# Attention with int8 query projection: the query made transposed, keys and queries stacked through DRAM

## The chip, the cores and the metric

The kernel runs on one core of a Trainium2 chip. The metric is the device time in microseconds of one launch. PE is the matrix engine (PEld its weight loads), DVE the vector engine, ACT the scalar engine, POOL the general-purpose engine and SP the engine that issues nearly all transfers. A value in f32 that is to be multiplied at better than the rounded precision is split into a rounded part "hi" and a rest "lo"; a product is then three matmuls (hi·hi, hi·lo, lo·hi) or, where the inner size is only 32, one matmul over a stack of three 32-row pieces.

## The reference, cut to what matters

There are 32 batches of 112 tokens with 512 channels, 16 heads of 32, and a context of 375 rows a batch. The linear maps for q and for the output quantise both operands to integers in -127..127.

```python
def _w8a8_linear(x, w, b):
    qx, sx = _dyn_quant(x)            # a scale for each token
    qw, sw = _quant_weight(w)         # a scale for each output channel
    y = jnp.einsum('bnc,oc->bno', qx, qw) * (sx * sw[:, 0])
    return y + b
q = _w8a8_linear(x, wq, bq).reshape(B, N, H, D).transpose(0, 2, 1, 3)
k = (cond @ wk.T + bk).reshape(B, L, H, D).transpose(0, 2, 1, 3)
v = (cond @ wv.T + bv).reshape(B, L, H, D).transpose(0, 2, 1, 3)
scores = jnp.einsum('bhnd,bhld->bhnl', q, k) * inv_sqrt_d + mask[:, None]
attn = jax.nn.softmax(scores, axis=-1)
o = jnp.einsum('bhnl,bhld->bhnd', attn, v)
return _w8a8_linear(o, wo, bo)
...
x = x + attention(_layernorm(x), ctx_2048, mask)
x = x + ffn(_layernorm(x))            # 8 experts, top 2 of them a token
```

## The kernel before

The program has four stages, one after the other: `prepare_weights` (weights of q and of the output quantised and turned, those of k and v split), `attention`, `route` and `experts`. The change touches the first two.

`attention` is a software pipeline over the batches, written by hand. Iteration `it` runs the heads of batch `it` (scores, softmax, turned probabilities, values), prepares batch n = `it`+1 (its projections of k and v, its q), loads and normalises x of batch `it`+2, and finishes the batches `it`-1 and `it`-2 (output projection, second normalisation, router). Every engine runs its own list of instructions, ordered by the head number h = 0..15; between engines only semaphores count. Each engine's list is executed strictly in its order, SP's list of transfers too. Iterations -1 and before only fill the pipeline, iterations 32 and 33 empty it, and iteration 31 has no next batch to prepare.

The path of q of batch n, before. DVE quantises the normalised x to `x_int` (112 tokens in partitions) at h = 14 of the iteration before. PE turns it at h = 6 (L603), DVE clips it to `x_int_t`, and PE multiplies at h = 7 (L638): four bf16 matmuls with 512 columns, tokens in partitions. DVE multiplies by the token's scale (one number a partition) and the row `wq_row` at h = 8 (L498), POOL adds `bq_row` (L357), PE turns the result at h = 9 with four f32 transposes (L603), ACT rounds it to `q_hi` out of `misc` at h = 9 (L424), and DVE makes `q_lo` at h = 10 (L502). Now the channels are in partitions, four groups of 128, which are four heads of 32 rows each.

A score is one matmul over 96 rows, so SP gathers 32-row pieces: `k_stack` holds k_hi, k_lo, k_hi and `q_stack` q_hi, q_hi, q_lo. `stack_keys(half)` issues 12 transfers for eight heads (L279), from SBUF to SBUF, each of 32 partitions and two heads; two halves a batch. The queries take 12 more (L316). That is 36 transfers a batch on SP, besides the twelve others (weights of the experts that are split on the way in four parts, mask, x, context, results). The first half of the keys of batch n may be overwritten once the eighth score of `it` is done, the second half once all sixteen are.

The lines that bind one engine to the other here: `scores` on PE waits for `k_stacked` and `q_stacked` at h = 0 and for `k_stacked` at h = 8; ACT waits for `k_stacked` before it overwrites `k_hi` and for `q_stacked` before it overwrites `q_hi`.

## Time and profile before

| | |
|---|---|
| median of 3 runs | 1607.95 us (1605.15 to 1608.63) |
| profiled execution, its own time | 1609.71 us |
| its span, first to last instruction | 1608.0 us |
| PE busy | 1494.6 us, 93% of the span |
| DVE, ACT, POOL busy | 897.5, 884.0, 660.6 us |
| mean granted clock of PE | 0.965 of full |

Full speed of PE is 2.4 GHz, and the other level that occurs is half of it. Matmuls overlap in the record, so the sum of their durations says less than the distance from one start to the next. In the rows below a time is in microseconds from the start of the span.

### The profile page before, as it was taken

Reading aid. Unit: us, or ns where it says so; the run is one execution under the profiler, and the core shown is the slowest. Engines: PE = TensorE matmul, PEld = TensorE weight load, DVE = VectorE, ACT = ScalarE, POOL = GpSimd, SP = SyncE. Lnnn points to the kernel's source line nnn. Section 1 sums busy time; section 2 is a strip of 40 time slices with the busy share of each in tenths; the row PEclk is TensorE's granted clock in tenths of the full one; section 3 lists DMA queues with packets and bytes.
Section 4 is the critical chain, followed back from the end, with each engine's and each line's share of the span. In section 5 each row is a group of like instructions: output and inputs, shape, how many; then the busy total and the mean of one; then the engine's idle time right before and its main releaser. Section 6 shows DMA issues by size and latency. Waiting matters only on the chain. (4 is left out here: it accounts for less than half of the span.)

```text
span 1608.0 us, 40123 instructions
## 1 busy us (share of the span) xinstructions
PE 1494.6 (93%) x11594; PEld 1317.6 (82%) x11595; DVE 897.5 (56%) x2365; ACT 884.0 (55%) x2097; POOL 660.6 (41%) x671
## 2 busy tenths in 40 slices
PE   2899999999999999999999999984399999999896
PEld 2788888888888888888888888873299999999895
DVE  6557666766676667666766676654632222222221
ACT  2467667677777776777677767761033333333232
POOL 4233334333443234323432343323555555656453
PEclk9999999999999999999999999985599999999998
DMA  5567777677767776777677767654537776666643
GB/s 173 145 170 196 209 200 197 179 228 205 194 178 226 202 196 179 225 205 196 178 225 201 200 179 222 185 142 141 160 68 186 182 175 134 148 154 125 160 77 48
DMA packets 220124, 281.09 MB, mean 175 GB/s; under 512 B 83568, under 2 KB 164976, under 8 KB 220080
## 3 DMA queue, kind: packets, MB, share of 16 engines
q1 hardware_dynamic: 203952, 247.24, 54.3%
q0 software_dynamic: 16128, 33.30, 11.6%
q8 instruction: 23, 0.38, 0.1%
q14 instruction: 21, 0.17, 0.0%
HBM read 118.31 MB, written 66.17 MB: 115 GB/s over the span
## 5 line engine op out<-in xcount | busy, mean ns | idle before, releaser
L464 DVE CUSTOM_DVE_ANT_0 probs<-score,neg_mask 112x375 f32<-112x375 f32 x512 | 279.7, 546 | 254.8 <-PE score L555 251.5
L392 ACT ACTIVATE probs<-probs,neg_max 112x375 f32<-112x375 f32 x512 | 312.3, 610 | 197.2 <-DVE neg_max L464 191.7
L563 PE MATMUL turn<-ident,probs 112*125 112x112 f32 x1536 | 264.8, 282 | 2.8 <-ACT probs L392 2.5
L385 ACT ACTIVATE probs_t<-turn 125x336 f32<-125x336 f32 x512 | 226.0, 441 | 71.6 <-PE turn L563 70.6
L563 PEld LDWEIGHTS turn<-ident,probs 112*125 112x125 f32 x1536 | 227.2, 190 | 36.4 <-issue 14.4
L555 PE MATMUL score<-k_stack,q_stack 96*112 96x376 f32 x512 | 209.4, 409 | 8.5 <-DMA q_stack<-q_lo 6.2
L591 PE MATMUL proj<-ctx_hi,wk_hi 128*128 128x376 f32 x512 | 176.0, 344 | 1.9 <-PEq L29 1.1
L591 PE MATMUL proj<-ctx_lo,wk_hi 128*128 128x376 f32 x512 | 172.0, 336 | 0.0
L591 PE MATMUL proj<-ctx_hi,wk_lo 128*128 128x376 f32 x512 | 171.7, 335 | 0.0
L1032 DVE TENSOR_TENSOR a_lo<-a_ps,a_hi 128x384 fp32r<-128x384 f32 x63 | 35.1, 557 | 243.7 <-ACT a_hi L1007 243.7
L596 PE MATMUL proj<-wv_hi,ctx_hi 128*125 128x512 f32 x384 | 151.8, 395 | 0.0
L596 PE MATMUL proj<-wv_hi,ctx_lo 128*125 128x512 f32 x384 | 151.7, 395 | 0.0
L596 PE MATMUL proj<-wv_lo,ctx_hi 128*125 128x512 f32 x384 | 151.0, 393 | 0.0
L354 POOL TENSOR_SCALAR neg_mask<-neg_mask 112x375 f32<-112x375 f32 x32 | 16.8, 525 | 305.2 <-DMA neg_mask<-mask 305.2
L370 POOL TENSOR_TENSOR ctx_lo<-ctx_stage,ctx_hi 128x1504 fp32r<-128x1504 f32 x31 | 106.6, 3437 | 57.9 <-ACT ctx_hi L429 57.9
L990 POOL DMA_INDIRECT out<-y_rows,scatter_idx x63 | 101.9, 1618 | 57.3 <-POOL scatter_idx L986 50.7
L375 POOL TENSOR_TENSOR w_raw<-w_raw,w_hi 128x1056 fp32r<-128x1056 f32 x32 | 78.9, 2467 | 92.9 <-ACT w_hi L434 92.9
L591 PEld LDWEIGHTS proj<-ctx_hi,wk_hi 128*128 128x128 f32 x512 | 97.4, 190 | 8.7 <-issue 1.5
L1020 ACT ACTIVATE y_rows<-y_ps,row_share 128x512 f32<-128x512 f32 x63 | 43.5, 691 | 106.7 <-PE y_ps L1102 73.3
L555 PEld LDWEIGHTS score<-k_stack,q_stack 96*112 96x112 f32 x512 | 92.4, 181 | 9.9 <-issue 7.5
L591 PEld LDWEIGHTS proj<-ctx_lo,wk_hi 128*128 128x128 f32 x512 | 97.6, 191 | 0.0
L591 PEld LDWEIGHTS proj<-ctx_hi,wk_lo 128*128 128x128 f32 x512 | 96.9, 189 | 0.0
(198 smaller groups left out, 3393.9 us busy)
## 6 DMA issues: line engine op xcount, KB each, us to landing
k_stack<-k_hi SPq DMA_DIRECT2D x512, 94.0 KB, 2.2
k_stack<-k_lo SPq DMA_DIRECT2D x256, 94.0 KB, 2.2
ctx_stage<-ctx_t SPq DMA_DIRECT2D x32, 750.0 KB, 5.0
q_stack<-q_hi SPq DMA_DIRECT2D x256, 56.0 KB, 2.0
w_raw<-gate_up_t SPq DMA_DIRECT2D x32, 352.0 KB, 3.1
gate_up_dram_hi<-w_hi SPq DMA_DIRECT2D x32, 352.0 KB, 4.8
gate_up_dram_lo<-w_raw SPq DMA_DIRECT2D x32, 352.0 KB, 5.2
gate_up_hi<-gate_up_dram_hi SPq DMA_DIRECT2D x16, 704.0 KB, 4.9
```

The lines of the kernel that those rows point to most:

```text
L370: pool.tensor_tensor(c_lo[:, par % 2, :, :], stage[:, :, :], c_hi[:, par % 2, :, :].bitcast(F32), ALU.subtract).then_inc(c_lo_made, 1)
L375: pool.tensor_tensor(w_lo[:, :], w_raw[:, :], w_hi[:, :].bitcast(F32), ALU.subtract).then_inc(w_lo_made, 1)
L385: act.activation(probs_t[:, h % RING_T, :, :], turn[h % 2][0:LC, 0:LT * N].rearrange("p (l n) -> p l n", l=LT), ACT.Copy).then_inc(turned_ ...
L392: act.activation(probs[:, h % DS, :], probs[:, h % DS, :], ACT.Exp, bias=neg_max[:, par % 2, h:h + 1], scale=-1.0, accum_out=total[:, par ...
L464: dve.tensor_tensor_reduce(probs[:, h % DS, :], score[h % 2][0:N, 0:L], neg_mask[:, p, :], 1.0, BIG, ALU.add, ALU.min, neg_max[:, p, h:h + ...
L555: pe.matmul(score[h % 2][0:N, 0:LP], q_st[:, par % 2, h, :], k_st[:, h, :], start=True, stop=True).then_inc(scored, 1)
L563: mm = pe.transpose(turn[h % 2][0:LC, l * N:(l + 1) * N], probs[:, h % DS, l * LC:(l + 1) * LC], W["ident"][0:N, 0:N])
L591: mm = pe.matmul(bank[:, 0:LP], W[w][:, t, 128 * u:128 * u + 128], c[:, q, t, :], start=(t == 0 and w == "wk_hi" and c is c_hi), stop=(t = ...
L596: mm = pe.matmul(bank[0:LC, :], c[:, q, t, l * LC:(l + 1) * LC], W[w][:, t, :], start=(t == 0 and w == "wv_hi" and c is c_hi), stop=(t == ...
L990: pool.indirect_dma_start(out, bass.IndirectOffsetOnAxis(ap=si[par][:, 0:1], axis=0), y[:, par, :], None, compute_op=ALU.add).then_inc(sca ...
L1020: act.activation(y[:, other, :], y_ps[other][:, 0:C], ACT.Copy, scale=share[:, other:other + 1]).then_inc(y_made, 1)
L1032: dve.tensor_tensor(a_lo[:, :], a_ps[:, 0:FP], a_hi[:, :].bitcast(F32), ALU.subtract).then_inc(a_lo_made, 1)
```

## The change

q is made with the channels in partitions from the start: for each of the four channel groups four matmuls whose weights are a 128x128 piece of `wq_int` and whose moving operand is the turned `x_int_t` with 112 columns. The token's scale then varies along the free axis, so it is needed as a row in every partition: SP stores the 112 scales of batch `it`+2 to DRAM (`x_scales`) at the end of iteration `it`, fetches them back as a broadcast row in the next iteration, and POOL multiplies them by the channels' scale `wq_col` into `q_scale`. DVE multiplies by `q_scale`, POOL adds the column `bq_col`, and ACT and DVE split `q_t` out of SBUF instead of out of PSUM. The four f32 transposes at h = 9 go.

Keys and queries are kept as one tile of both parts (`k_parts`, `q_parts`), stored to DRAM (one transfer a half of the keys, one for the queries) and fetched back in three transfers each, one for each third of the stack. In all 12 transfers a batch take the place of 36, and two more move the scale. The heads lie in the stack in the order h % 4 * 4 + h // 4. ACT waits for `k_kept` and `q_kept` (stored) where it waited for the stacks. In `prepare_weights` the row `wq_row` (four spread activations, four f32 matmuls, one copy) goes, and the row `bq_row` becomes a column. DVE's list gets 14 semaphore increments ahead of its loop.

```diff
@@ prepare_weights, PE @@
-                pe.wait_ge(spread_done, KT * (i + 1))
-                if i:
-                    pe.wait_ge(row_out, i)
-                for t in range(KT):
-                    mm = pe.matmul(ps[0:N, 128 * t:128 * t + 128], spread[:, i, t, :], W["ident"][:, :],
-                                   start=True, stop=True)
-                mm.then_inc(row_made, 1)
+            pe.wait_ge(spread_done, KT)
+            for t in range(KT):
+                mm = pe.matmul(ps[0:N, 128 * t:128 * t + 128], spread[:, t, :], W["ident"][:, :],
+                               start=True, stop=True)
+            mm.then_inc(row_made, 1)
...
@@ attention, SP @@
-            def stack_keys(half):
-                for i in range(4):
-                    rows = slice(QUARTER * i, QUARTER * i + QUARTER)
-                    for r, src in ((0, k_hi), (1, k_lo), (2, k_hi)):
-                        sp.dma_start(k_st[QUARTER * r:QUARTER * r + QUARTER, 8 * half + i:8 * half + 8:4, :].bitcast(F32),
-                                     src[rows, 2 * half:2 * half + 2, :].bitcast(F32)).then_inc(k_stacked[half], 16)
+            def keep_keys(b, half):
+                sp.dma_start(k_dram[b, half, :, :, :], k_parts[:, :, 2 * half:2 * half + 2, :].bitcast(F32).rearrange("p a g l -> p a (g l)")).then_inc(k_kept[half], 16)
+            def stack_keys(b, half):
+                for r, part in ((0, 0), (1, 1), (2, 0)):
+                    sp.dma_start(k_st[QUARTER * r:QUARTER * r + QUARTER, :, :].bitcast(F32).rearrange("p (i g) l -> p i g l", g=G4)[:, :, 2 * half:2 * half + 2, :],
+                                 k_dram[b, half, :, part, :].rearrange("(i p) (g l) -> p i g l", p=QUARTER, g=2)).then_inc(k_stacked[half], 16)
...
                 if has_a:
-                    need(sp, unit_out, UNITS * it + KT)
+                    need(sp, k_kept[1], 16 * (it + 1))
                     if inside or it > 0:
                         waited(sp)
                         need(sp, scored, H * it)
-                    stack_keys(1)
+                    stack_keys(it, 1)
...
+                if has_n:
+                    need(sp, x_scale_stored, 16 * (n + 1))
+                    need(sp, q_scaled, n)
+                    sp.dma_start(x_scale_row[:, :], x_scales[n, :].rearrange("(a t) -> a t", a=1).to_broadcast([128, N])).then_inc(x_scale_in, 16)
...
                     need(sp, unit_out, UNITS * n + KT // 2)
+                    keep_keys(n, 0)
+                    need(sp, k_kept[0], 16 * (n + 1))
                     if has_a:
                         waited(sp)
                         need(sp, scored, H * it + H // 2)
-                    stack_keys(0)
+                    stack_keys(n, 0)
+                    need(sp, unit_out, UNITS * n + KT)
+                    keep_keys(n, 1)
                     need(sp, q_out, 3 * n + 3)
-                    for i in range(4):
-                        rows = slice(QUARTER * i, QUARTER * i + QUARTER)
-                        for r, src in ((0, q_hi), (1, q_hi), (2, q_lo)):
-                            sp.dma_start(q_st[QUARTER * r:QUARTER * r + QUARTER, q, i:H:4, :].bitcast(F32),
-                                         src[rows, :, :].bitcast(F32)).then_inc(q_stacked, 16)
+                    sp.dma_start(q_dram[n, :, :, :], q_parts[:, :, :, :].bitcast(F32).rearrange("p a g n -> p a (g n)")).then_inc(q_kept, 16)
+                    need(sp, q_kept, 16 * (n + 1))
+                    for r, part in ((0, 0), (1, 0), (2, 1)):
+                        sp.dma_start(q_st[QUARTER * r:QUARTER * r + QUARTER, q, :, :].bitcast(F32).rearrange("p (i g) n -> p i (g n)", g=G4),
+                                     q_dram[n, :, part, :].rearrange("(i p) f -> p i f", p=QUARTER)).then_inc(q_stacked, 16)
...
+                if has_nn:
+                    nn = it + 2
+                    need(sp, ln1, 8 * nn + 5)
+                    with nc.allow_non_contiguous_dma(reason="one scale a token"):
+                        sp.dma_start(x_scales[nn, :].rearrange("(p a) -> p a", a=1), x_scale[:, par % 2:par % 2 + 1]).then_inc(x_scale_stored, 16)
...
@@ attention, POOL @@
+                    need(pool, x_scale_in, 16 * (n + 1))
+                    need(pool, q_out, 3 * n)
+                    pool.tensor_tensor(q_scale[:, :, :], x_scale_row[:, :].unsqueeze(1).to_broadcast([128, G4, N]),
+                                       W["wq_col"][:, :].unsqueeze(2).to_broadcast([128, G4, N]), ALU.mult).then_inc(q_scaled, 1)
                     need(pool, q_out, 3 * n + 2)
-                    need(pool, q_made, 3 * n)
-                    pool.tensor_tensor(q_tok[:, :], q_tok[:, :], W["bq_row"][0:N, :], ALU.add).then_inc(q_biased, 1)
+                    pool.tensor_tensor(q_t[:, :, :], q_t[:, :, :], W["bq_col"][:, :].unsqueeze(2).to_broadcast([128, G4, N]),
+                                       ALU.add).then_inc(q_biased, 1)
...
@@ attention, ACT, h == 9 @@
-                        need(act, q_made, 3 * n + 3)
-                        need(act, q_stacked, 16 * QDMAS * n)
-                        act.activation(q_hi[:, :, :], misc[:, 0:G4 * N].rearrange("p (g n) -> p g n", g=G4),
-                                       ACT.Identity).then_inc(q_hi_made, 1)
+                        need(act, q_biased, n + 1)
+                        need(act, q_kept, 16 * n)
+                        act.activation(q_hi[:, :, :], q_t[:, :, :], ACT.Identity).then_inc(q_hi_made, 1)
...
@@ attention, DVE, h == 8 and ahead of the loop @@
-                        dve.scalar_tensor_tensor(q_tok[:, :], misc[0:N, :], x_scale[:, q:q + 1], W["wq_row"][0:N, :],
-                                                 ALU.mult, ALU.mult).then_inc(q_out, 1)
+                        need(dve, q_scaled, n + 1)
+                        dve.tensor_tensor(q_t[:, :, :], misc[:, 0:G4 * N].rearrange("p (g n) -> p g n", g=G4), q_scale[:, :, :],
+                                          ALU.mult).then_inc(q_out, 1)
...
+            for _ in range(LOOP_OFFSET):
+                waited(dve)
...
@@ attention, PE, h == 7 and 9 @@
-                        for t in range(KT):
-                            mm = pe.matmul(misc[0:N, :], x_int_t[:, t, :], W["wq_int"][:, t, :], start=(t == 0), stop=(t == KT - 1))
+                        for g in range(G4):
+                            for t in range(KT):
+                                mm = pe.matmul(misc[:, g * N:(g + 1) * N], W["wq_int"][:, t, 128 * g:128 * g + 128], x_int_t[:, t, :],
+                                               start=(t == 0), stop=(t == KT - 1))
                         mm.then_inc(q_made, 1)
-                    if h == 9 and has_n:
-                        need(pe, q_biased, n + 1)
-                        turn_to_misc(lambda t: q_tok[:, 128 * t:128 * t + 128], W["ident"][0:N, 0:N], misc, N, 128).then_inc(q_made, 1)
```

On PE the order moves at h = 7 to 10. Before, in the first iteration with scores (L638 is the q product, L603 the transposes, L563 the turned probabilities, L555 the scores, L591 and L596 the projections of k and v):

```order
L638 MATMUL misc<-wq_int,x_int_t 112x512 x4
L563 MATMUL turn<-ident,probs 125x112 x3
L555 MATMUL score<-k_stack,q_stack 112x376
...
L596 MATMUL proj<-wv_hi,ctx_hi 125x512
L596 MATMUL proj<-wv_lo,ctx_hi 125x512
L596 MATMUL proj<-wv_hi,ctx_lo 125x512
L603 MATMUL misc<-ident,q_tok 128x112 x4
L563 MATMUL turn<-ident,probs 125x112 x3
L555 MATMUL score<-k_stack,q_stack 112x376
```

and now (L667 is the q product, L591 the turned probabilities, L583 the scores, L624 the projection of v):

```order
L667 MATMUL misc<-x_int_t,wq_int 128x112 x16
L591 MATMUL turn<-ident,probs 125x112 x3
L583 MATMUL score<-k_stack,q_stack 112x376
...
L624 MATMUL proj<-wv_hi,ctx_hi 125x512
L624 MATMUL proj<-wv_lo,ctx_hi 125x512
L624 MATMUL proj<-wv_hi,ctx_lo 125x512
L591 MATMUL turn<-ident,probs 125x112 x3
L583 MATMUL score<-k_stack,q_stack 112x376
```

Sixteen short matmuls stand in the place of four long ones, and nothing stands between the last projection of v of h = 9 and the turned probabilities of h = 10.

On SP one whole iteration, here iteration 2, which is written out ahead of the loop. Before, from the last transfer ahead of the keys on; the nine rows of keys of the second half that come before L292 read like the nine that follow L304:

```order
L292 DMA w_raw<-gate_up_t 128x704
L293 DMA w_raw<-down_t 128x352
L296 DMA neg_mask<-mask 112x375
L299 DMA out<-y 112x512
L301 DMA h_rows<-h_s 112x512
L304 DMA x_res<-x 112x512
L279 DMA k_stack<-k_hi 32x2x376
...
L316 DMA q_stack<-q_hi 32x4x112 x2
L316 DMA q_stack<-q_lo 32x4x112
...
L321 DMA ctx_stage<-ctx_t 128x4x375
L323 DMA x_in<-x 112x512
```

and now, from the row of the scales to the end of the iteration, less the four stores of the split expert weights (L341 and L342):

```order
L311 DMA x_scale_row<-x_scales 128x112
L314 DMA x_res<-x 112x512
L280 DMA k_parts_dram<-k_parts 256x1x752
L285 DMA k_stack<-k_parts_dram 32x4x752 x3
L280 DMA k_parts_dram<-k_parts 256x1x752
L327 DMA q_parts_dram<-q_parts 128x896
L330 DMA q_stack<-q_parts_dram 32x4x448 x3
L335 DMA ctx_stage<-ctx_t 128x4x375
L337 DMA x_in<-x 112x512
...
L347 DMA x_scales<-x_scale 112x1
```

The store of the second half of the keys stands behind the fetch of the first; the fetch of the queries stands directly behind their store, for which SP waits; the scales are stored last.

## Rows read from the trace of the kernel before

**Rows 1.** Stretches: busy us (count) of PE, PEld, DVE, ACT, POOL; clock; DMA share; GB/s.

```profile
59.18:1063.00 1003.82, 996.78 (x8590) 861.83 (x8591) 681.38 (x1925) 707.88 (x1759) 354.00 (x300) 1.00 0.71 197
579.58:611.85 32.27, 32.25 (x282) 27.78 (x281) 22.32 (x64) 23.02 (x57) 11.73 (x10) 1.00 0.73 198
557.00:558.00 1.00, 1.00 (x9) 1.00 (x7) 0.56 (x2) 1.00 (x4) 0.00 (x0) 1.00 0.65 153
...
59.00:65.00 6.00, 5.82 (x20) 5.84 (x21) 1.67 (x6) 2.21 (x6) 0.00 (x0) 0.50 1.02 283
```

**Rows 2.** What PE waited for, 62 to 1060 us: us in total, times, longest.

```profile
PE score L555 <- DMA q_stack<-q_lo: 2.6, 3, 1.3
PE misc L603 <- POOL q_tok L357: 1.8, 2, 1.4
PE score L555 <- issue: 1.7, 2, 1.3
```

**Rows 3.** PE in order of time: start, us, what, count.

```profile
560.32 0.37 PE L603 MATMUL misc<-ident,x_int 112*128 112x112 bf16 x4
560.53 0.54 PE L563 MATMUL turn<-ident,probs 112*125 112x112 f32 x3
...
561.59 1.02 PE L638 MATMUL misc<-wq_int,x_int_t 128*112 128x512 bf16 x4
562.46 0.48 PE L563 MATMUL turn<-ident,probs 112*125 112x112 f32 x3
...
565.40 0.40 PE L596 MATMUL proj<-wv_lo,ctx_hi 128*125 128x512 f32 x1
565.64 0.40 PE L596 MATMUL proj<-wv_hi,ctx_lo 128*125 128x512 f32 x1
565.98 0.60 PE L603 MATMUL misc<-ident,q_tok 112*128 112x112 f32 x4
566.42 0.49 PE L563 MATMUL turn<-ident,probs 112*125 112x112 f32 x3
```

**Rows 4.** Weight loads into misc: shortest, median, longest duration in ns.

```profile
L603 PEld LDWEIGHTS misc<-ident,x_int x128: 97/98/102, 43.8 to 1044.1; 112*128 112x128 bf16 x128
```

**Rows 5.** SP's issues in the same iteration: start, us to issue.

```profile
549.94 0.63 SPq L279 DMA_DIRECT2D k_stack<-k_hi  x1
...
561.47 0.73 SPq L279 DMA_DIRECT2D k_stack<-k_hi  x1
...
569.39 1.24 SPq L316 DMA_DIRECT2D q_stack<-q_hi  x2
...
577.40 0.42 SPq L321 DMA_DIRECT2D ctx_stage<-ctx_t  x1
```

**Rows 6.** Transfers: count, KB each, median us from issue to landing.

```profile
k_stack<-k_hi SPq DMA_DIRECT2D x512, 94.0 KB, 2.2
...
gate_up_dram_hi<-w_hi SPq DMA_DIRECT2D x32, 352.0 KB, 4.8
...
x_res<-x SPq DMA_DIRECT2D x32, 224.0 KB, 4.4
```

**Rows 7.** The path of q outside PE, in the same iteration.

```profile
563.80 0.74 DVE L498 SCALAR_TENSOR_TENSOR q_tok<-misc,x_scale,wq_row 112x512 f32<-112x512 f32 x1
...
564.63 1.29 POOL L357 TENSOR_TENSOR q_tok<-q_tok,bq_row 112x512 f32<-112x512 f32 x1 [1.61 <-DVE q_tok L498]
...
567.77 0.62 DVE L502 TENSOR_TENSOR q_lo<-misc,q_hi 128x448 fp32r<-128x448 f32 x1
```

**Rows 8.** The start: weights prepared, q of batch 0, the first score.

```profile
29.31 1.99 PE L156 MATMUL w_ps<-ident,w_spread 128*112 128x128 f32 x8
31.09 1.06 PE L149 MATMUL w_pt<-ident,w_ints 128*128 128x128 bf16 x8
...
49.19 0.62 DVE L502 TENSOR_TENSOR q_lo<-misc,q_hi 128x448 fp32r<-128x448 f32 x1 [0.22 <-ACT q_hi L424]
...
59.18 0.63 PE L555 MATMUL score<-k_stack,q_stack 96*112 96x376 f32 x1 [3.60 <-DMA q_stack<-q_lo]
```

More of the change, by code:

```diff
@@ L39, in prepare_weights @@
         ints = sb("w_ints", [128, 2, KT, C], BF16)
-        spread = sb("w_spread", [128, 2, KT, N])
+        spread = sb("w_spread", [128, KT, N])
         ones = sb("w_ones", [128, N])
@@ L97, in _ @@
             act.wait_ge(ident_made, 3)
-            for i in range(2):
-                act.wait_ge(scale_done, i + 1)
-                for t in range(KT):
-                    act.activation(spread[:, i, t, :], ones[:, :], ACT.Copy, scale=scale[:, i, t:t + 1]).then_inc(spread_done, 1)
+            act.wait_ge(scale_done, 2)
+            for t in range(KT):
+                act.activation(spread[:, t, :], ones[:, :], ACT.Copy, scale=scale[:, 1, t:t + 1]).then_inc(spread_done, 1)
             act.wait_ge(W["ctx_in"], 16)
@@ L104, in _ @@
             act.activation(W["c_hi"][:, 0, :, :], W["stage"][:, :, :], ACT.Identity).then_inc(W["c_hi_made"], 1)
-            for i, (_, _, row) in enumerate(pairs):
-                act.wait_ge(row_made, i + 1)
-                act.activation(row[0:N, :], ps[0:N, :], ACT.Copy, scale=-inv_sqrt_d if i == 0 else 1.0).then_inc(row_out, 1)
+            act.wait_ge(row_made, 1)
+            act.activation(W["wo_row"][0:N, :], ps[0:N, :], ACT.Copy).then_inc(row_out, 1)
         @block.vector
         def _(dve):
-            for i, (n, _, _) in enumerate(pairs):
+            for i, (n, _) in enumerate(pairs):
                 dve.wait_ge(loaded[n], 16)
@@ L128, in _ @@
                                       ALU.subtract).then_inc(ints_done, 1)
-            for i, (_, dst, _) in enumerate(pairs):
+            for i, (_, dst) in enumerate(pairs):
                 for t in range(KT):
@@ L189, in attention @@
         stage, c_hi, c_lo, x_in = W["stage"], W["c_hi"], W["c_lo"], W["x_in"]
-        k_hi, k_lo = sb("k_hi", [128, G4, LP], F32R), sb("k_lo", [128, G4, LP], F32R)
+        k_parts = sb("k_parts", [128, 2, G4, LP], F32R)
+        k_hi, k_lo = k_parts[:, 0, :, :], k_parts[:, 1, :, :]
         k_st = sb("k_stack", [96, H, LP], F32R)
-        q_hi, q_lo = sb("q_hi", [128, G4, N], F32R), sb("q_lo", [128, G4, N], F32R)
+        q_parts = sb("q_parts", [128, 2, G4, N], F32R)
+        q_hi, q_lo = q_parts[:, 0, :, :], q_parts[:, 1, :, :]
         q_st = sb("q_stack", [96, 2, H, N], F32R)
@@ L203, in attention @@
         x_int, x_int_t = sb("x_int", [N, C], BF16), sb("x_int_t", [128, KT, N], BF16)
-        q_tok = sb("q_tok", [N, C])
+        q_t = sb("q_t", [128, G4, N])
+        x_scale_row, q_scale = sb("x_scale_row", [128, N]), sb("q_scale", [128, G4, N])
         out_ts = sb("out_ts", [128, G4, N])
@@ L547, in _, with stacked_at @@
         def _(pe):
+            def stacked_at(h):
+                return h % 4 * G4 + h // 4
             def scores(b, par, h):
@@ L554, in scores @@
                 need(pe, masked, k - 1)
-                pe.matmul(score[h % 2][0:N, 0:LP], q_st[:, par % 2, h, :], k_st[:, h, :],
+                pe.matmul(score[h % 2][0:N, 0:LP], q_st[:, par % 2, stacked_at(h), :], k_st[:, stacked_at(h), :],
                           start=True, stop=True).then_inc(scored, 1)
@@ L636, in body @@
                         need(pe, q_out, 3 * n + 1)
[L637 to L638 removed]
+                        for g in range(G4):
+                            for t in range(KT):
+                                mm = pe.matmul(misc[:, g * N:(g + 1) * N], W["wq_int"][:, t, 128 * g:128 * g + 128], x_int_t[:, t, :],
+                                               start=(t == 0), stop=(t == KT - 1))
                         mm.then_inc(q_made, 1)
[L640 to L642 removed]
                     if h == 11 and has_m:
```

37 lines of the change are left out of this document (20 added, 17 removed).

## The prediction

> **What bounds the kernel now.** I read first the stretches, then what PE waited for, then PE in order of time. In one iteration of the attention loop, 32.27 us long, PE is busy for 32.25 us, while ACT has 23.0, DVE 22.3 and POOL 11.7 us of work, and the transfer engines are busy for 0.73 of the time [rows 1]. The whole stretch from the first score to iteration 31 is 1003.8 us, or 32.4 us for each of its 31 iterations. PE's waits between 62 and 1060 us come to 6.1 us in these rows [rows 2], and the same view by shorter stretches has all of them in the first five iterations. After those the loop costs what its matmuls cost on PE, by start-to-start distance, and a microsecond taken from PE's list in one iteration counts 31 times, as long as no other chain closes up. After 1063 us the change touches nothing that carries time.
>
> The second nearly full resource is SP's list. In the iteration shown the 12 transfers of a half of the keys take from 561.47 to 569.39 and the 12 of the queries from there to 577.40, 7.9 and 8.0 us [rows 5]: 0.66 us for each issue, 23.9 us for all 36, and 12 other issues beside them. The queries are issued just before the next iteration's first score, at 579.58. That is why the waits of the first iterations are mostly for `q_stack`.
>
> **The change, part by part.** All sums are against the profiled execution's own 1609.71 us.
>
> (a) The transposes at h = 9. The last two matmuls of v start at 565.40 and 565.64, so the next could start at 565.88; the turned probabilities behind the transposes start at 566.42 [rows 3]. The transposes, with the wait for POOL's bias ahead of them, take 0.54 us. Removed from 31 iterations: 16.7 us. In iteration -1 they lie in front of a wait of 3.60 us [rows 8] and count nothing in PE's own order.
>
> (b) The q product. Before, 561.59 to 562.46, 0.87 us for four matmuls with 512 columns [rows 3]. Now 16 with 112 columns, each with its own 128-column bf16 weights. The trace has just this shape in the transposes of `x_int`: four from 560.32 to 560.53, 0.21 us, 0.0525 us each [rows 3]. 16 make 0.84 us: a gain of 0.03 an iteration, 0.9 us in all. From above, if the weight loads of 98 ns [rows 4] hid under nothing, 16 would take 1.57 us, a loss of 0.70 an iteration. From below 112 columns at the rate of the 512 (0.2175 us each) are 0.048 us, 0.76 in all. I take 0.84, since shape and type are the same.
>
> The Trainium skill speaks against it (TensorE: Matmul & The Clock Gate, Back-to-back issue gap): streams of weight load and matmul are said to sustain about 81 ns a matmul with 128 columns and 131 ns with 512. By it the product would go from 0.52 to an estimated 1.30 us. The rows have 0.87 for the first of these, and 52.5 ns for the short shape, so the sum goes by the rows.
>
> (c) The other engines' steps. DVE multiplies 128x448 in place of 112x512, about 0.65 for 0.74 us, POOL's bias is 1.13 for 1.29, by 448/512 of [rows 7], and POOL has a new product of the same size, 1.13 us more on 11.7. ACT's rounding no longer waits for PE. DVE and ACT have over 9 us of room an iteration. Cost nothing; the cover is PE's full list.
>
> (d) SP's list. 36 issues become 12, two small ones come in: some 22 x 0.66 = 14.5 us of SP's time come free in an iteration. In the steady loop that is worth nothing, as PE waits for none of it. In the first iterations it removes the lateness of the queries: of the 6.1 us in [rows 2] I take 5.5 (from 0, if new waits replace them, to 6.1).
>
> (e) The weights' stage. Of the f32 matmuls with `w_spread` at 29.31 the q part goes: until the next transposes at 31.09 that is 1.8 us [rows 8], on the chain transposes, output weights, last copy. 1.8 us.
>
> (f) The start of the loop. `q_lo` of batch 0 ends at 49.81 and the first score starts at 59.18 [rows 8], 9.4 us, of which 8 are SP's 12 issues. Now: a store, a wait, three fetches. A transfer lands after 2.2 us from SBUF to SBUF with 94 KB, and 4.8 us for a 352 KB store to DRAM beside others [rows 6]; the 448 KB store lies between, about 3.6, then two more issues of 0.66 and a last fetch of about 3. In all 7.9: a gain of 1.5 us (-1.6 to 3.7, with 4.8 or 2.2 for both).
>
> Sum: 16.7 + 0.9 + 5.5 + 1.8 + 1.5 = 26.4 us. The median lies 1.8 us below the profiled execution; taken from it, 1607.95 - 26.4 = 1581.6.
>
> **The new waits, and their room.** The iteration in the rows begins at 547.3 and the next at 579.58 [rows 1]. Keys, second half: stored in the iteration before, fetched from about 550, where their first issue stands now [rows 5], and needed at h = 8, at 562.5 [rows 3]. Room some 5 us. Keys, first half: fetch cannot start before the eighth score (561.4), as now [rows 5], needed at 579. Room over 10.
>
> The scales. Their fetch stands behind the second result store on SP, which needs DVE's h = 3, so at about 555.5; with 4.4 us to land as the neighbouring `x_res` has [rows 6] and 1.13 us on POOL the product is there at 561.1. DVE needs it at 563.80 [rows 7]. Room 2.7 us, and a late `q_t` first has to use up the room of the queries. Behind the waiting POOL instruction stand the bias, `x_res` and the norm of the next batch, all with room.
>
> The queries are the tight one. `q_lo` ends at 568.4 [rows 7]; PE wants them at 579.0 in the shorter iteration: 10.6 us for what took 9.4 at the start before and which I price at 7.9. Room 2.7 us. But the store now runs behind the keys' store, and the bytes grow: each iteration moves 2.0 MB more (1.54 of keys, 0.46 of queries) on 6.4 (198 GB/s by 32.27 us), 266 GB/s over 31.7 us. At 153 GB/s of 32-partition fetches the engines were busy for 0.65 [rows 1], so such fetches end near 235 GB/s, and all in all I get a DMA share near 0.95.
>
> **The rivals.**
>
> *Queries late (slower).* If a store and a last fetch each take the 4.8 us of the loaded store, the chain is 4.8 + 1.3 + 4.8 = 10.9 us, 0.3 over. If the 32-partition fetches out of DRAM run only at the 153 GB/s seen, 0.69 MB of queries take 4.5 us instead of 2.9 and the 1.16 MB of keys ahead 7.5 instead of 4.9, which pushes the store: 4.2 us more, 1.5 over the room. A stall of 1.5 us is 46 us in 31 iterations: 1582 + 46 = 1628. It decides from a chain of 11.2 us on, where the stall (0.6) eats (a) and (b). For it speaks the queue of bytes, against it that rows before have 283 GB/s in a crowded stretch [rows 1]. The Trainium skill (SBUF — State Buffer, Door 1: The DMA port swizzle) says that 32 partitions reach only half of the 16 ports. By its 436 GB/s for all I estimate 218 for such a fetch; the share of 0.65 at 153 GB/s agrees.
>
> *Weight loads not hidden.* (b) at its upper bound costs 0.70 an iteration, 21.7 us, in place of the 0.9 gained: 1582 + 22.6 = 1604.
>
> *Scales late.* Above 2.7 us of lateness DVE stands at h = 8, and its later scores with it. A fetch of 8 us would leave some 1 us of stall an iteration: 1582 + 31 = 1613.
>
> *The gain is hidden.* If the chain of score, DVE maximum, ACT exponential and turned probabilities closes up, only (e), (f) and part of (d) stay: 1608 - 8 = 1600. Against it: ACT 23.0 of 32.27.
>
> **How the numbers follow.** Forecast 0.72; queries late 0.13 (a third of it a small stall that leaves a gain); weight loads 0.06; scales late 0.04; hidden 0.05. The likeliest case alone is 1574 to 1592: 3.4 us below its sum if the half clock between 59 and 65 us [rows 1] does not come back once the wait of 3.6 us before the first score shrinks, 10 above if (d) gives nothing and (f) goes wrong. With the weight loads, the hidden gain and the small stalls the range is 1573 to 1604. Within 0.2%, 3.2 us, is about what a measurement of this kernel can tell from no change. Faster: 0.72, hidden 0.05, most of the weight loads 0.04, small stalls 0.04, 0.85. Slower: 0.11. Same: 0.04.
>
> **What would show it.** Right: an iteration of about 31.7 us with PE at 100%; the 16 matmuls 0.84 us from first start to next; no wait of a score for `q_stack` after the first iteration; SP waiting some 14 us an iteration more. Wrong: PE waits for `q_stack` in every iteration; a pitch of 80 to 98 ns in the q product; DVE waiting for POOL's `q_scale`; a DMA share of 1.

## The result, and the profile after

The changed kernel takes 1807.22 us (median of 4 runs, 1800.99 to 1808.19), the kernel before 1608.29 beside it: ratio 1.1231, interval 1.12 to 1.1262. It is 12% slower. The profiled execution took 1806.98 us, its span is 1805.2 us. The sum of the prediction, 1582, is 225 us too low. The experiments below split this into 153 us that go with the form of the scales' store, 46 us by which the kernel without that harm is still slower than the one before, and the 26 us of gain that did not come.

The stretches of the changed kernel; columns as in [rows 1]:

```profile
62.00:1256.00 1194.00, 1054.21 (x8841) 928.34 (x8841) 680.60 (x1927) 703.61 (x1762) 380.05 (x331) 0.93 0.82 220
609.68:645.58 35.90, 33.41 (x289) 29.43 (x289) 22.31 (x63) 23.02 (x57) 12.29 (x11) 0.94 0.86 233
...
644.00:651.00 7.00, 5.42 (x19) 5.38 (x20) 1.78 (x5) 2.08 (x7) 1.28 (x1) 0.57 1.04 346
645.60:647.00 1.40, 1.40 (x5) 1.35 (x6) 0.50 (x3) 0.00 (x0) 0.00 (x0) 0.50 0.99 281
...
653.00:654.00 1.00, 1.00 (x36) 0.83 (x24) 0.00 (x0) 0.15 (x1) 0.62 (x2) 1.00 0.28 87
```

An iteration that was full of PE work [rows 1] is now 35.90 us long in this example, with PE busy for 33.41. Two other things stand in the rows: a granted clock under 1, and a stretch in which the transfer engines are busy for only 0.28 of the time, though transfers of SP's are still on the way. The loop itself ends near 1256 us instead of 1063.

What PE waited for between 65 and 1265 us (us in total, times, longest):

```profile
PE score L583 <- DMA q_stack<-q_parts_dram: 94.7, 27, 8.5
PE score L583 <- issue: 18.8, 5, 4.8
PE misc L631 <- DVE o_int L471: 10.4, 11, 1.2
PE misc L655 <- ACT h_t L442: 8.3, 5, 3.2
PE proj L619 <- DVE k_parts L512: 5.5, 4, 1.9
```

The first two are one wait, that of the first score for its queries: 113.5 us where [rows 2] had 4.3. These five rows make 137.7 us. The rest is the clock: 0.93 over 1194 us, with 1.2 and 2.4 GHz as its two levels, is an estimated 167 us at the lower, in which half, about 84 us, is lost. Together 222 us, against a span that is 197 us longer than before and 224 longer than the forecast. The lower level follows the wait: PE is idle for 2.5 us before the score at 645.58, the next 1.4 us run at 0.50, and between 644 and 651 the mean is 0.57, that is, about 6 of the 7 us at the lower level.

What SP waited for, same stretch; the number behind each wait is again us in total, times, longest:

```profile
SPq L330 <- DMA q_parts_dram<-q_parts: 228.1, 31, 8.9
SPq L298 <- DMA down_dram_lo<-w_raw: 221.9, 25, 11.7
SPq L255 <- DMA k_parts_dram<-k_parts: 152.8, 31, 7.4
```

Three waits, 603 us, for a store to land. Two I had seen coming, those of the queries and of the keys. The middle one is the wait of the raw expert weights' load for the last store of the split ones; that edge existed before, and the change's diff does not touch it.

One iteration of SP, issue by issue (start, us to issue):

```profile
608.37 0.39 SPq L342 DMA_DIRECT2D down_dram_lo<-w_raw  x1
609.14 0.34 SPq L347 DMA_DIRECT2D x_scales<-x_scale  x1
609.67 2.15 SPq L285 DMA_DIRECT2D k_stack<-k_parts_dram  x3
620.24 0.35 SPq L298 DMA_DIRECT2D w_raw<-gate_up_t  x1
...
624.20 0.57 SPq L280 DMA_DIRECT2D k_parts_dram<-k_parts  x1
629.81 1.32 SPq L285 DMA_DIRECT2D k_stack<-k_parts_dram  x3
631.37 0.55 SPq L280 DMA_DIRECT2D k_parts_dram<-k_parts  x1
632.20 0.38 SPq L327 DMA_DIRECT2D q_parts_dram<-q_parts  x1
640.05 1.30 SPq L330 DMA_DIRECT2D q_stack<-q_parts_dram  x3
...
645.59 0.55 SPq L347 DMA_DIRECT2D x_scales<-x_scale  x1
646.98 1.40 SPq L285 DMA_DIRECT2D k_stack<-k_parts_dram  x3
657.38 0.35 SPq L298 DMA_DIRECT2D w_raw<-gate_up_t  x1
```

Read it from the top. The last weight store is issued at 608.37, and the load that waits for it leaves at 620.24, 11.9 us later; before, a store of this group landed after 4.8 us [rows 6]. Between the two stand only the scale store and the keys' fetch. In the next iteration it is the same, and there the window 653 to 654 shows the transfer engines busy for 0.28. Everything behind is late by that much: the keys' first half at 624.20, its fetch at 629.81. Then the queries: DVE's subtraction for `q_lo` starts at 631.3 and takes 0.62 us; the store of both parts is issued at 632.20 and has landed at 640.05, and the score starts at 645.58. From the end of `q_lo` that chain is 13.6 us, where 10.6 were to be had.

The scales' row is late as well. Its fetch is issued at 622.96, 13.3 us after the first score of the iteration, where the prediction had 8.2. DVE then stands before its product with `q_scale`, 65 to 1265 us:

```profile
DVE q_t L521 <- POOL q_scale L376: 53.7, 27, 4.7
```

Landings of the changed kernel, 62 to 1256 us (count, KB each, median us from issue to landing):

```profile
k_stack<-k_parts_dram SPq DMA_DIRECT2D x187, 376.0 KB, 5.4
k_parts_dram<-k_parts SPq DMA_DIRECT2D x62, 752.0 KB, 6.8
...
q_stack<-q_parts_dram SPq DMA_DIRECT2D x96, 224.0 KB, 3.7
q_parts_dram<-q_parts SPq DMA_DIRECT2D x31, 448.0 KB, 7.9
```

The matmuls did what was forecast. PE in order of time (start, us, what, count):

```profile
625.19 0.33 PE L619 MATMUL proj<-ctx_hi,wk_lo 128*128 128x376 f32 x1
625.37 0.96 PE L667 MATMUL misc<-x_int_t,wq_int 128*128 128x112 bf16 x16
626.16 0.54 PE L591 MATMUL turn<-ident,probs 112*125 112x112 f32 x3
```

16 matmuls in 0.79 us from the first's start to the next work, 49 ns each. Where the transposes stood, the turned probabilities now start 0.24 us after the last matmul of v (629.40 to 629.64), one ordinary distance.

### The profile page after: what moved, and what is told of

Its sections match the earlier page's. It is cut to its first block and busy times, and to the rows that moved or that the text cites. A ratio compares the mean times of both kernels' runs of the same rounds, so it can differ in the third digit from the quotient of the medians.

```text
span 1805.2 us, 40617 instructions
## 1 busy us (share of the span) xinstructions
PE 1552.8 (86%) x11842; PEld 1384.6 (77%) x11843; DVE 896.5 (50%) x2366; ACT 877.0 (49%) x2092; POOL 687.4 (38%) x703
## 5 line engine op out<-in xcount | busy, mean ns | idle before, releaser
L583 PE MATMUL score<-k_stack,q_stack 96*112 96x376 f32 x512 | 227.1, 443 | 115.0 <-DMA q_stack<-q_parts_dram 94.7
L591 PE MATMUL turn<-ident,probs 112*125 112x112 f32 x1536 | 281.5, 296 | 5.3 <-ACT probs L415 5.3
L591 PEld LDWEIGHTS turn<-ident,probs 112*125 112x125 f32 x1536 | 248.0, 205 | 31.6 <-issue 10.5
L619 PE MATMUL proj<-ctx_hi,wk_hi 128*128 128x376 f32 x512 | 194.9, 381 | 8.7 <-DVE k_parts L512 7.6
L583 PEld LDWEIGHTS score<-k_stack,q_stack 96*112 96x112 f32 x512 | 101.2, 198 | 120.9 <-issue 117.5
L619 PE MATMUL proj<-ctx_lo,wk_hi 128*128 128x376 f32 x512 | 188.4, 368 | 0.0
L619 PE MATMUL proj<-ctx_hi,wk_lo 128*128 128x376 f32 x512 | 187.5, 366 | 0.0
L624 PE MATMUL proj<-wv_hi,ctx_hi 128*125 128x512 f32 x384 | 152.8, 398 | 3.1 <-DVE k_parts L512 3.1
L624 PE MATMUL proj<-wv_hi,ctx_lo 128*125 128x512 f32 x384 | 152.4, 397 | 0.0
L624 PE MATMUL proj<-wv_lo,ctx_hi 128*125 128x512 f32 x384 | 152.1, 396 | 0.0
L619 PEld LDWEIGHTS proj<-ctx_hi,wk_hi 128*128 128x128 f32 x512 | 112.4, 220 | 17.7 <-DVE k_parts L512 9.2
L363 POOL TENSOR_TENSOR y<-y,x_res 112x512 f32<-112x512 f32 x32 | 40.9, 1278 | 219.2 <-DVE y L492 219.2
L619 PEld LDWEIGHTS proj<-ctx_lo,wk_hi 128*128 128x128 f32 x512 | 111.7, 218 | 0.0
L619 PEld LDWEIGHTS proj<-ctx_hi,wk_lo 128*128 128x128 f32 x512 | 109.9, 215 | 0.0
```

Source lines behind the costliest of these rows:

```text
L583: pe.matmul(score[h % 2][0:N, 0:LP], q_st[:, par % 2, stacked_at(h), :], k_st[:, stacked_at(h), :], start=True, stop=True).then_inc(scored, 1)
L591: mm = pe.transpose(turn[h % 2][0:LC, l * N:(l + 1) * N], probs[:, h % DS, l * LC:(l + 1) * LC], W["ident"][0:N, 0:N])
L619: mm = pe.matmul(bank[:, 0:LP], W[w][:, t, 128 * u:128 * u + 128], c[:, q, t, :], start=(t == 0 and w == "wk_hi" and c is c_hi), stop=(t = ...
L624: mm = pe.matmul(bank[0:LC, :], c[:, q, t, l * LC:(l + 1) * LC], W[w][:, t, :], start=(t == 0 and w == "wv_hi" and c is c_hi), stop=(t == ...
```

## Experiments

There were two suspects, the store of the scales (112 writes of 4 bytes into one piece of 448 bytes) and the stacks' way through DRAM, and a third question: whether the shorter PE list is worth anything. All times are medians; "before" is the kernel before on the same chip. It took 1604 to 1610 us in the five groups of runs, so a difference between runs of different groups is good to some 5 us only.

| run | scales | keys | queries | us | ratio to before (95%) |
|---|---|---|---|---|---|
| changed kernel | 4-byte store | DRAM | DRAM | 1807.22 | 1.12 to 1.1262 |
| e1_no_scale_store | none | DRAM | DRAM | 1653.81 | 1.023 to 1.0305 |
| e1_scale_own_rows | 4-byte, own rows | DRAM | DRAM | 1657.65 | 1.024 to 1.0317 |
| e4_after_turned_scale | 4 x 128 bytes | DRAM | DRAM | 1654.61 | 1.0242 to 1.0346 |
| e1_stacks_only | q as before | DRAM | DRAM | 1636.23 | 1.0088 to 1.0191 |
| e1_local_stacks | 4-byte store | SBUF | SBUF | 1664.77 | 1.0268 to 1.0386 |
| e3_before_plus_store | q as before, 4-byte store | SBUF | SBUF | 1659.31 | 1.0301 to 1.0368 |
| e2_local_no_store | none | SBUF | SBUF | 1608.76 | 1.0005 to 1.0036 |
| e2_scale_by_pe | by PE | SBUF | SBUF | 1610.92 | 1.002 to 1.0059 |
| e2_only_queries_dram | none | SBUF | DRAM | 1583.74 | 0.983 to 0.9902 |
| e2_only_keys_dram | none | DRAM | SBUF | 1586.57 | 0.9851 to 0.9926 |
| e3_pe_scale_q_dram | by PE | SBUF | DRAM | 1591.65 | 0.9879 to 0.9925 |
| e3_turned_scale_q_dram | 4 x 128 bytes | SBUF | DRAM | 1594.15 | 0.9885 to 0.993 |

### The scale store taken away, or its writes spread (e1_no_scale_store, e1_scale_own_rows)

The first drops the store and fetches the broadcast row from x instead, so that values of x stand in for the token scales. The second keeps 112 writes of 4 bytes, but gives each a DRAM row of its own, 512 bytes apart; its row too is fetched from x.

```diff
-sp.dma_start(x_scales[nn, :].rearrange("(p a) -> p a", a=1), x_scale[:, ...])   # both
+sp.dma_start(x_scales[nn, :, 0:1], x_scale[:, ...])                             # own rows only
-... x_scales[n, :] ... to_broadcast([128, N])
+... x[n, 0, 0:N] ... to_broadcast([128, N])
```

> The changed kernel without the store of the token scales; the row is fetched from x instead, so the scales of q are wrong ones and only the time counts. Theory 1 (the 112 writes of 4 bytes hold up the transfer queue for some 7 us an iteration, so the stores of the expert weights land late, the loads, the first half of the keys and the queries follow late): the attention loop falls to about 32 us an iteration and the whole to 1580 to 1620 us. Theory 2 (the 2 MB more an iteration and the fetches into 32 partitions out of DRAM are too slow by themselves): the time stays within 30 us of 1807.

> The scales are stored, each into a DRAM row of its own of 512 bytes, and the row is fetched from x as in the run without the store, so the scales of q are wrong ones. Theory 1a (the small writes disturb because they fall on the same 448 bytes): as without the store, 1580 to 1620 us. Theory 1b (each write of 4 bytes costs, wherever it falls): about 1800 us. Theory 2: about 1807 us.

1653.81 and 1657.65 us, both above the 1580 to 1620 of the expectation that had the store as the one cause: the store costs some 150 us here, and only in the form in which all its writes lie in one small piece. The waits of PE and of SP without the store, 65 to 1100 us:

```profile
PE score L577 <- DMA q_stack<-q_parts_dram: 35.0, 24, 3.5
PE score L577 <- issue: 11.6, 4, 3.2
```

```profile
SPq L329 <- DMA q_parts_dram<-q_parts: 194.1, 30, 8.0
SPq L255 <- DMA k_parts_dram<-k_parts: 130.8, 31, 5.7
SPq L298 <- DMA down_dram_lo<-w_raw: 109.0, 30, 4.9
```

The weights' wait falls from 8.9 us a time (221.9 in 25) to 3.6 (109.0 in 30). The waits for keys and queries fall only from 4.9 and 7.4 us to 4.2 and 6.5, and the first score is still late by 1.5 us an iteration. So there are two causes, and one is left.

### The transposed q with the old stacks, and the new stacks with the old q (e1_local_stacks, e1_stacks_only)

```diff
 # e1_local_stacks: 24 + 12 transfers from SBUF to SBUF as before, scales stored and fetched as in the change
-KDMAS, QDMAS = 3, 3
+KDMAS, QDMAS = 12, 12
 # e1_stacks_only: the kernel before with k_parts, q_parts and the 12 transfers through DRAM
-KDMAS, QDMAS = 12, 12
+KDMAS, QDMAS = 3, 3
```

> q made transposed with the scales through DRAM, but keys and queries stacked from SBUF to SBUF by 36 transfers a batch as before. Theory 1: the small writes still hold up the queue, the weights' stores land late and SP's full list gets later still: 1650 to 1850 us. Theory 2: with the DRAM stacks gone the transposed q is worth its 17 us: 1585 to 1595 us.

> q made as before (tokens in partitions, transposes, no scales through DRAM), keys and queries stacked through DRAM by the 12 transfers. Theory 1: no small writes, so the queue keeps up: 1595 to 1620 us. Theory 2: the DRAM stacks are the trouble: 1750 to 1830 us.

1664.77 and 1636.23 us: each half of the change is slower by itself than the kernel before (1609.89 us beside them), by 55 and by 26 us. For the second 1595 to 1620 us had been expected with the small writes as the one cause, so that is not the one cause either. In e1_stacks_only PE's first score waits 21 us in all for its queries, where it waits 46.6 in e1_no_scale_store, which has the transposed q besides. With both stacks through DRAM the transposed q thus costs 18 us (1636.23 to 1653.81) in place of a gain. The transposed q leaves a shorter iteration for the same chain and puts the fetch of the row on SP's list; which of these it is, no run took apart.

### The store alone, on the kernel before (e3_before_plus_store)

```diff
+if has_nn:
+    need(sp, ln1, 8 * nn + 5)
+    sp.dma_start(x_scales[nn, :].rearrange("(p a) -> p a", a=1), x_scale[:, ...]).then_inc(x_scale_stored, 16)
```

> The kernel before with one thing added: the store of 112 token scales, 4 bytes each, into one 448-byte piece of DRAM, at the end of SP's body; nothing fetches it, so the extra store changes nothing in the output. If such a store is dear by itself (my theory, since with each scale in a DRAM row of its own the changed kernel lost about 150 us of its time), what SP queues behind it (the raw weights' loads of the next iteration and the queries' transfers) lands 4 to 6 us later, and the time goes to 1630 to 1700 us. If the store is only dear where the bytes of keys and queries through DRAM keep the rings full, this run stays within 1605 to 1620 us (one more issue of 0.6 us on SP each iteration).

1659.31 us, 51 more than before (1608.31 beside it). PE's waits between 65 and 1100 us:

```profile
PE misc L610 <- POOL q_tok L364: 15.2, 16, 3.8
PE score L562 <- DMA k_stack<-k_hi: 11.7, 10, 3.4
PE score L562 <- DMA q_stack<-q_lo: 5.3, 6, 2.2
```

These waits make 32 us of the 51; the rest was not taken apart. SP has a wait that the kernel before does not have in its loop:

```profile
SPq L293 <- DMA down_dram_lo<-w_raw: 24.1, 16, 2.8
```

Nothing reads what is stored, and no instruction waits for it inside the loop; it is paid for by the transfers around it, here the last store of the weights, which SP issues just before it. Its rival, that the store hurts only where keys and queries through DRAM fill the queues, falls. Against the kernel before beside them, e1_local_stacks and e2_local_no_store (below) differ by 50 us too. So the store costs some 50 us where the stacks are made inside SBUF, and 150 where the landing of other stores is on the path three times an iteration. Not all of the 50 need be the form of the store: it is also one more issue, 0.65 us in the median, on a list of SP that has only 28 us to spare in 995 (below), by my estimate up to 20 us in 31 iterations. No run stored the scales in own rows or in four pieces beside stacks that are both made in SBUF.

### Is the shorter PE list worth its price? (e2_local_no_store, e2_only_queries_dram, e2_only_keys_dram)

All three have the transposed q and no scale store (values of x stand in for the token scales). The first has both stacks inside SBUF; each of the others sends one of them through DRAM.

```diff
 # e2_only_queries_dram against e2_local_no_store
-for i in range(4):
-    for r, src in ((0, q_hi), (1, q_hi), (2, q_lo)):
-        sp.dma_start(q_st[...], src[rows, :, :])
+sp.dma_start(q_dram[n, :, :, :], q_parts[:, :, :, :]).then_inc(q_kept, 16)
+need(sp, q_kept, 16 * (n + 1))
+for r, part in ((0, 0), (1, 0), (2, 1)):
+    sp.dma_start(q_st[...], q_dram[n, :, part, :])
```

> Both suspects taken away: keys and queries stacked from SBUF to SBUF, and the scales not stored (the row comes from x, so q's scales are wrong ones). Theory 1 (two separate costs, the shared small writes and the longer queue of the DRAM stacks): what is left is the transposed q, worth 17 to 20 us, 1588 to 1595 us. Theory 3 (something in the q path itself costs, POOL's new product or the order of the waits): 1605 us or more.

> Queries stacked through DRAM, keys from SBUF to SBUF, no store of the scales. If the queue of bytes ahead of the queries (1.16 MB of keys fetched into 32 partitions and 0.77 MB stored) is what makes them late, this is nearly as fast as the version with both local, 1585 to 1600 us. If the round trip of the queries is too long by itself, 1620 us or more.

> Keys stacked through DRAM, queries from SBUF to SBUF in 12 transfers, no store of the scales. If the keys' traffic ahead in the queue sets the queries' landing, they are late here too, since 8 us of issuing come on top: 1610 to 1650 us. If only the queries' own round trip mattered, 1585 to 1595 us.

1608.76, 1583.74 and 1586.57 us, beside 1604.29 for the kernel before. The first has PE's list shorter by the 17.6 us of (a) and (b) and gains none of it, against the expected 1588 to 1595. The view that explains it is SP's waits, for the kernel before from 65 to 1060 us,

```profile
SPq L279 <- PE score L555: 18.9, 34, 1.9
SPq L327 <- POOL w_raw L375: 6.5, 19, 0.8
```

and of e2_local_no_store, 65 to 1100 us.

```profile
SPq L283 <- PE score L571: 15.3, 26, 1.5
SPq L334 <- POOL w_raw L386: 14.4, 2, 14.0
```

In the 995 us of the first SP waits for 28 in all; its list is 97% full. (Of the 14.4 us in the last line 14.0 are one wait at the end of the loop.) A full list of SP reaches PE by a detour, which DVE's waits show, 65 to 1100 us, first e2_local_no_store, then e2_only_queries_dram:

```profile
DVE q_t L509 <- POOL q_scale L364: 74.1, 31, 3.6
DVE q_t L509 <- POOL q_scale L364: 25.8, 24, 2.2
```

The scales' row is fetched late on the full list, POOL's product and with it DVE come late, and PE waits 22.6 us between 65 and 1060, of which 14.1 are for DVE's `o_int`; with the queries through DRAM it waits 7.9. PE and SP are both the bound, and a step off PE's list pays only if SP's list gets shorter too. With 12 query issues turned into 4 it does, and 25 us appear. That the path of the transposed q costs by itself, the rival in the expectation, falls, since 1583.74 us has the same path. The number of issues and the way through DRAM change together in these runs, so that it is the number is argued from SP's waits. Either stack may go through DRAM for that, but not both. With the keys through DRAM and the queries in 12 transfers inside SBUF the time is 1586.57 us, not the 1610 to 1650 expected: small transfers behind the keys' bytes landed after 3.0 us in the median. SP in e2_only_queries_dram:

```profile
550.14 0.37 SPq L320 DMA_DIRECT2D q_parts_dram<-q_parts  x1
552.64 1.31 SPq L323 DMA_DIRECT2D q_stack<-q_parts_dram  x3
```

The queries' store has landed after 2.5 us, which is also its median there. With the keys ahead of it, and still without the scale store, the same store takes 6.7 us in the median and 7.9 in this iteration of e1_no_scale_store:

```profile
621.85 1.35 SPq L285 DMA_DIRECT2D k_stack<-k_parts_dram  x3
623.45 0.55 SPq L280 DMA_DIRECT2D k_parts_dram<-k_parts  x1
624.28 0.39 SPq L326 DMA_DIRECT2D q_parts_dram<-q_parts  x1
632.21 1.30 SPq L329 DMA_DIRECT2D q_stack<-q_parts_dram  x3
```

Ahead of it stand 1.155 MB of keys (three times 376 KB of 1024 bytes), fetched into pieces of 32 partitions, and a store of 0.770 MB (752 KB). The change's own trace gives their rates:

```profile
633.00:636.00 3.00, 3.00 (x19) 2.68 (x20) 1.80 (x5) 1.82 (x5) 2.42 (x1) 1.00 1.05 220
636.00:638.00 2.00, 2.00 (x12) 1.67 (x11) 1.90 (x7) 0.85 (x3) 1.00 (x1) 1.00 1.00 358
```

220 GB/s while the fetches fill the rings, 358 once the 128-partition store is under way. 1.155 MB at 220 GB/s are 5.3 us and 0.770 at 358 are 2.2 us, 7.4 in all, of which some has gone when the queries' store is issued; the queries' own 0.459 MB at 358 then take 1.3. Counted from the keys' fetch at 629.81, this estimate ends at 638.5, and the queries' store had landed by 640.05. The trace agrees with the Trainium skill (SBUF — State Buffer, Door 1: The DMA port swizzle), from whose half of the ports I had estimated 218 GB/s.

### A scale without small writes (e2_scale_by_pe, e3_pe_scale_q_dram, e3_turned_scale_q_dram, e4_after_turned_scale)

Two ways, each in the full function. Either ACT spreads the scale over 128 columns and one f32 matmul against the identity makes the row in every partition, with no transfer; or DVE turns the scale in blocks of 32, and four pieces of 128 bytes are stored and fetched as a row.

```diff
 # by PE, at h = 2 (e2: DVE's product at h = 3; e3: at h = 2)
+pe.matmul(misc[:, 0:N], x_scale_wide[:, :], W["ident"][0:N, 0:N], start=True, stop=True)
 # turned
+dve.transpose(x_scale_t[:, p, :], x_scale[:, p, :])
+sp.dma_start(x_scales[nn, :].rearrange("(p a) -> p a", a=32), x_scale_t[0:128:32, par % 2, :])
```

> A version that could beat both: transposed q, stacks from SBUF to SBUF as before, and the row of the scales made by one f32 matmul of the spread scale with the identity (0.2 us on PE) at h = 2, with no transfer of scales at all. An iteration should fall from 32.27 to some 31.9 us: 1608 - 31 x 0.37 - 1.8 = 1595 us, range 1588 to 1603.

> The full function: the queries made transposed, their scale row made on chip by one f32 matmul (0.31 us on PE) right before the product, keys stacked inside SBUF as before, queries stacked through DRAM. With the queries alone through DRAM and no scale made the time was 1583.7 us; the matmul, its eviction and one pitch more add 0.4 to 0.6 us an iteration, 31 times 12 to 19 us at most: 1590 to 1602 us. If SP's list is what held the same scale path with SBUF stacks at 1610.9, this run must be at least 10 us below that; if the scale path itself held it (k_lo late behind DVE's scale), it stays at 1605 to 1612 us.

> The full function: the token scale turned on VectorE so that it leaves as four pieces of 128 bytes, instead of 112 writes of 4 bytes, fetched back as a row an iteration later; keys stacked inside SBUF as before, queries stacked through DRAM. Theory (the 4-byte writes into the same 448 bytes cost about 150 us of the changed kernel's time, keys and queries together through DRAM the other 50): nothing of either is left and the gain that was predicted from PE's steps shows, 1583 to 1595 us. If it is any store of the scale ahead of the weights' loads that stalls the queue, whatever its pieces, 1620 us or more.

> The changed kernel whole, keys and queries both through DRAM, with one edit: the token scale leaves as four pieces of 128 bytes instead of 112 writes of 4 bytes into the same 448 bytes. Theory: the small writes cost what the run with a DRAM row for each scale gave back, so 1645 to 1665 us; what is then left over the kernel before, about 45 us, is the wait for queries behind the bytes of keys. Rival, any store of the scale at that place stalls the queue when the rings are full of keys' bytes: 1700 us or more.

1610.92, 1591.65, 1594.15 and 1654.61 us. The first has both stacks in SBUF and gains nothing, against the expected 1588 to 1603; the second is the same with the queries through DRAM and 19 us faster. That the first meets SP's list again is argued and not shown: it has no transfer of scales, and SP waits 40 us there for PE's scores. The two differ in DVE's place of the scale product too, so not all of the 19 us need be SP's. The last is the changed kernel with nothing but the scale's store in another form, and it gives back 153 us. Its PE waits, 65 to 1100 us:

```profile
PE score L588 <- DMA q_stack<-q_parts_dram: 33.8, 24, 3.4
PE score L588 <- issue: 9.9, 4, 3.2
```

These are 44 us, about as without any store (46.6): a store of the scale is free there if its pieces are few. With only the queries through DRAM it is not quite, 1594.15 beside 1583.74 us without a store, though on two chips. The best version of the full function is e3_pe_scale_q_dram, 1591.65 us (1591.24 to 1592.56), 1.0% under the kernel before; e3_turned_scale_q_dram, 1594.15 (1587.66 to 1596.24), can't be told from it.

## Why the prediction was wrong

**(a) and (b), PE's list: right.** The transposes are gone from PE's rows, and 16 matmuls take 0.79 us for the 0.84 forecast. The figure of the Trainium skill that I had weighed against it (TensorE: Matmul & The Clock Gate, Back-to-back issue gap, 81 ns for such a pair) is contradicted by the rows, 49 ns. The rival "weight loads not hidden" is out.

**(c), the other engines: nearly right in cost, shown by e2_only_queries_dram,** where a gain of 20.6 us (1583.74 beside a before of 1604.29) stands for the 26.4 of the sum. DVE's waits for `q_scale`, at nothing in the sum, are 25.8 us even there, and PE waits 7.9 us in all.

**(d), SP's list: two errors.** The first is "two small ones come in": the scale's store was counted as one issue of 0.66 us, by its 448 bytes. It cost 153 us in the changed kernel (e4_after_turned_scale, with the same bytes in four pieces) and 51 on the kernel before. This is the step that failed, and no rival of mine held it. "Scales late" priced the row's arrival, not what the store does to its neighbours. That rival came true as well, DVE waiting 53.7 us for `q_scale`, but as something that follows from SP's late list: with the scales in four pieces it waits 2.8 us (e4_after_turned_scale). How much of the 153 us goes by that way, no run shows. The second is "In the steady loop that is worth nothing": SP's list, 97% full, was as much the bound as PE's. With the stacks left alone (a) and (b) would have been worth nothing (1608.76). I had called SP's list nearly full and had not drawn the consequence. The change did free the list, so this error cost the sum nothing.

**"The new waits, and their room", the queries: the term was mis-sized.** I priced the chain from `q_lo` to score at 7.9 us with 10.6 to be had. It is 13.6 us in the changed kernel and, in the iteration of e1_no_scale_store shown above (`q_lo` ends at 624.1, the score starts at 637.98), 13.9 also without the scale store. The store's 3.6 us were 7.9 there and 6.7 in that run's median, because a full half of keys, fetched and stored, stands ahead of it; the last fetch's 3 us plus issues were 5.5. I had named both pieces, and set the room of the queries against landings that the kernel before had only beside lighter traffic. Without the store's harm this puts the kernel 46 us over the one before and 70 over e2_only_queries_dram, which differs from e1_no_scale_store only in the keys' way (1653.81 against 1583.74, on two chips). The keys' way is thus shown as the cause; that it works by the bytes ahead of the queries is argued from the landings and rates above.

**The rival "Queries late"** had this mechanism, and a stall of 1.5 us an iteration, which is just what PE's waits show without the scale store (46.6 us over 31). It gave 1628 us against the measured 1654. What it left out is the clock, 0.98 on average in e1_no_scale_store between 62 and 1060 us, by estimate some 40 us at half speed and about 20 lost. Not every wait is followed by the lower level. In that run one of 1.54 us before the score at 603.24 is not, and one of 2.86 before that at 637.98 is:

```profile
603.20:605.00 1.80, 1.76 (x11) 1.62 (x11) 1.07 (x3) 0.39 (x1) 0.00 (x0) 1.00 1.01 275
637.90:640.00 2.10, 2.02 (x8) 1.98 (x9) 1.10 (x3) 0.41 (x1) 0.00 (x0) 0.50 1.01 364
```

I gave this rival 0.13. In the changed kernel the two faults meet: the late weights' loads make the keys' first half late, its transfers fall upon the queries', the wait grows to 3.7 us an iteration, and the clock to 0.93.

**(f), the start of the loop: right only with the keys in SBUF.** From the end of `q_lo` to the first score, 9.4 us before and 7.9 forecast, e2_only_queries_dram takes 8.3 (48.32 to 56.57) and e4_after_turned_scale, with the keys through DRAM too, 14.1 (48.21 to 62.31). In the changed kernel the first score starts at 69.2 in place of 59.18. (e) was not taken apart. The lower end of the likeliest case was added up wrongly: 3.4 us below 1581.6 is 1578, not 1574.

How 112 small writes hold up a queue was not settled. The runs show that neither the bytes nor the number nor the size of the writes does it (own rows cost nothing in the changed kernel), so it is that they share one piece of 448 bytes. That they wait for one another there is my reading of it. The Trainium skill (DMA: Bandwidth & Descriptors, Specifications) says that a write under 512 bytes becomes a read, a change and a write back; by that alone own rows and 128-byte pieces would cost alike to the shared piece, and they do not, though writes of this sort to the same bytes could well have to follow one another, which no run shows. Nor did a run spread the 4-byte writes by less than 512 bytes, so the spacing at which the harm ends stays open. Another order of SP's list in the changed kernel, with the queries' store ahead of the keys' transfers, was not tried.

## What to carry to other kernels

Before a step is taken off a full engine, read the waits of the issuing engine too: a list of transfers that hardly waits is a second bound, and hides whatever the first gives back. Price a round trip through DRAM not by its own bytes but by all that stands in the queue ahead of it, at the rate of those transfers, and send one of two tensors that way rather than both. And do not store a column of scalars element by element into one small piece of memory: turn it first, or make the row on chip.

## What the hardware showed that I had not expected

- A store of 448 bytes as 112 writes of 4 bytes costs 153 us over 32 batches where other landings are on the path, and 51 where nothing waits for it, of which up to 20 may be its mere issue. In the first of these kernels the same writes 512 bytes apart, or the same bytes in four pieces, cost nothing that these runs can tell. Behind it the transfer engines were busy for 0.28 of a microsecond at 87 GB/s, with SP waiting for a store issued ahead of it.
- PE idle for 2.5 us in a loop that is otherwise full is followed by about 6 us at the lower level of the clock, which lose 3 more: this wait is paid about twice. A wait of 1.54 us was followed by none.
- 112-column bf16 matmuls, each with a weight load of its own, run at 49 ns each.
